# Low halves of the routed rows made by VectorE instead of GpSimd, and GpSimd's loop over the scatters without other work in it

## The reference

```python
h = _L0_tok_ref(x, tok_w, tok_b)            # keep 88 of 125 tokens in each of 32 batches
h = h + _L0_attn_ref(_layernorm(h), ...)    # attention with quantised activations
h = h + _L0_ffn_ref(_layernorm(h), ...)

def _L0_ffn_ref(x, scale, gate_w, gate_b, w1, b1, w2, b2):   # E = 16 experts, K = 4
    t = xf * rsqrt(mean(xf * xf) + EPS) * scale
    g = t @ gate_w.T + gate_b
    vals, idx = top_k(g, K)
    w = softmax(vals) / K
    full_w = zeros((T, E)).at[arange(T)[:, None], idx].set(w)
    h = _swiglu(einsum('th,ehf->tef', t, w1) + b1)
    y = einsum('tei,eih->teh', h, w2) + b2
    return x + einsum('teh,te->th', y, full_w) * K
```

## Time and profile before

| | us |
|---|---|
| median of 3 runs | 892.26 |
| lowest, highest run | 891.8, 892.93 |
| the profiled execution's own time | 891.94 |
| its span | 890.2 |

### The profile page before, as it was taken

One profiled execution on the slowest core, in us unless ns is written; L12 is line 12 of the kernel. 1 busy time (PEld: TensorE's weight loads), 2 busy tenths in 40 slices (PEclk: granted clock), 3 DMA queues, 4 the chain that ended last, 5 costly groups with the idle time before them and its releaser, 6 DMA issues.

```text
span 890.2 us, 16237 instructions
## 1 busy us (share of the span) xinstructions
PE 414.2 (47%) x4049; PEld 283.5 (32%) x4050; DVE 646.5 (73%) x1921; ACT 514.6 (58%) x838; POOL 480.5 (54%) x598
## 2 busy tenths in 40 slices
PE   0476454545454544442230001007887977888300
PEld 0232232323232322222120001005766766766200
DVE  4684769898999898999774226005988978988376
ACT  0242599999999999998520005005665655665200
POOL 8452525554545463626137777771877666776600
PEclk9987655555555555555555555557999998999655
DMA  8499080637271814000001111223434333332186
GB/s 177 51 261 284 2 266 10 186 91 218 58 226 48 259 38 144 1 1 1 0 10 60 65 63 60 76 72 80 115 98 114 92 93 89 96 99 69 27 286 211
DMA packets 102393, 93.37 MB, mean 105 GB/s; under 512 B 14822, under 2 KB 96493, under 8 KB 102338
## 3 DMA queue, kind: packets, MB, share of 16 engines
q1 hardware_dynamic: 88938, 72.87, 29.5%
q0 software_dynamic: 10272, 17.70, 5.8%
q10 hardware_dynamic: 3128, 2.16, 0.8%
HBM read 35.21 MB, written 61.24 MB: 108 GB/s over the span
## 4 chain that ended last, share of the span: by engine, by line
DVE 27%; issue 23%; ACT 19%; PE 12%; POOL 10%; DMA 4%; SPq 3%; DVEq 1%; POOLq 0%; ACTq 0%
POOL region L610 8%; PE pS L1589 3%; DVE S_rho L1091 2%; DMA S_e<-expert_rows 2%; ACT S_sq L784 2%; ACT arena L720 2%; DVE S_ratio L1071 2%; ACT L784 2%; DVE xsel L1349 2%; ACT S_sq L789 2%; DVE arena L1324 2%; ACT pTs L772 2%; DVE stage L1303 2%; DVE arena L1294 2%; PE pP L1589 2%
## 5 line engine op out<-in xcount | busy, mean ns | idle before, releaser
L635 POOL DMA_INDIRECT expert_rows<-stage,dest x118 | 117.8, 998 | 30.0 <-issue 29.1
L610 POOL DMA_INDIRECT region<-arena,slots x96 | 93.9, 979 | 31.7 <-issue 28.1
L491 POOL TENSOR_TENSOR w1s<-stage,w1s 128x384 f16<-128x384 f32 (+17 forms) x72 | 69.7, 968 | 15.1 <-POOL w1s L491 6.3
L582 POOL CAST oq<-o 128x384 bf16<-128x384 int8 x24 | 20.3, 846 | 97.6 <-ACT o L751 97.6
L628 POOL TENSOR_TENSOR stage<-arena,stage 128x256 f16<-128x256 f32 x59 | 40.9, 693 | 52.1 <-ACT stage L849 51.9
L1407 PE MATMUL pX<-arena,WA 128*128 128x384 f16 x86 | 35.3, 514 | 52.0 <-ACT arena L720 49.3
L1613 PE MATMUL pX<-w2s,stage 128*128 x472 | 57.6, 253 | 3.4 <-DVE avE L1305 1.7
L849 ACT ACTIVATE stage<-arena 128x256 f16<-128x256 f32 x59 | 24.6, 417 | 59.0 <-DVE arena L1324 59.0
L1598 PE MATMUL pO<-idh,arena 128*128 128x128 f16 x354 | 31.3, 228 | 50.4 <-DMA arena<-region 49.4
L562 POOL CAST arena<-arena 128x384 bf16<-128x384 int8 x42 | 27.6, 671 | 41.0 <-ACT arena L720 41.0
L808 ACT ACTIVATE arena<-arena 128x576 f16<-128x576 f32 x8 | 5.5, 682 | 75.7 <-DMA region<-arena,slots 71.9
(11 more groups left out here) (356 smaller groups left out, 1833.8 us busy)
## 6 DMA issues: line engine op xcount, KB each, us to landing
region<-zrow SPq DMA_DIRECT2D x45, 800.0 KB
arena<-region SPq DMA_DIRECT2D x59, 200.0 KB
stage<-expert_rows SPq DMA_DIRECT2D x16, 384.0 KB, 4.8
stage<-in_L_ffn_w_dram SPq DMA_DIRECT2D x24, 192.0 KB
stage<-in_L_ffn_w_dram SPq DMA_DIRECT2D x8, 384.0 KB
arena<-in_x_dram SPq DMA_DIRECT2D x4, 672.0 KB
expert_rows<-stage,dest POOLq DMA_INDIRECT x118
out_dram<-xsel ACTq DMA_DIRECT2D x8, 198.0 KB
```

The costliest lines, as they stand in the source:

```text
L491: pool.tensor_tensor(ws[rows, min(kind + 1, 3), two, to:to + width], st[rows, :, at:at + width], ws[rows, kind, two, to:to + width], ALU.s ...
L610: pool.indirect_dma_start(region_rows, bass.IndirectOffsetOnAxis(ap=slots[r][:, i, m:m + 1], axis=0), rows[r][:, i, :].bitcast(I16), None, ...
L635: pool.indirect_dma_start(y_dram, bass.IndirectOffsetOnAxis(ap=dest[(st - 7) % 8][:, j:j + 1], axis=0), ysb[b][:, j, :], None, bounds_chec ...
```

## The change

The two low halves of each group are made on DVE, at a place in DVE's loop between `evac_tT(q-1)` and `top_experts(q-2)`. POOL's loop holds the scatters alone, group after group. Waits, buffers, operands and shapes are the same.

```diff
@@ pool @@
-            def low_rows(q):
-
-                pool.wait_ge(s["high2"], q + 1)
-                low_halves(pool, rows[q % 4], tn[q % 2], s["low2"])
-
             def scatter_rows(q):
...
             pool.wait_ge(s["rows_zeroed"], 16 * NFILL + 64)
-            for q in range(NQ + 3):
-                if q < NQ:
-                    low_rows(q)
-                if q >= 3:
-                    scatter_rows(q - 3)
+            for q in range(NQ):
+                scatter_rows(q)
@@ vector @@
+            def low_rows(q):
+
+                dve.wait_ge(s["high2"], q + 1)
+                low_halves(dve, rows[q % 4], tn[q % 2], s["low2"])
+
             def evac_tT(q):
...
                     norm_rows(q)
                 if 1 <= q < NQ + 1:
                     evac_tT(q - 1)
+                if q < NQ:
+                    low_rows(q)
                 if 2 <= q < NQ + 2:
                     top_experts(q - 2)
                 if q >= 3:
                     find_slots(q - 3)
```

## The result

The changed kernel takes 902.7 us in the median of four runs (901.3 to 904.2), the kernel before beside it 892.0 (890.3 to 892.9). The ratio is 1.0122, with a 95% interval of 1.0100 to 1.0144: slower by 10.7 us. The profiled execution took 902.8 us, with a span of 900.7.

A forecast was written before the change was run, and what follows sets the result against it. The stretch of POOL's 96 scatters was taken to bound the kernel's route; four gaps longer by 3.08 us (+12.3) and the start (+1.1) made +13.4, so 905.6 us, range 901.8 to 908.8.

The forecast's parts named there:

- The mechanism: At groups 1 to 4, DVE's wait for high2 stands ahead of the slots POOL needs, so four gaps remain, each longer.
- The terms of the gap: Between groups on POOL: landing 1.45, ACT 0.68, handover 0.05, halves 0.83, experts and slots 2.95, issue 0.90; 6.86 instead of 3.78 us.
- Halves: In each gap, the pair of low halves on DVE takes 0.83 us, bounds 0.6 and 1.4.
- Experts and slots: In each gap, top_experts and find_slots on DVE up to slots_ready take 2.95 us, bounds 2.8 and 3.1.
- Issue: In each gap, POOL's issue from slots written to first transfer lies open: 0.90 us, bounds 0.75 and 0.98.
- The start: Before the first scatter, DVE's added halves lengthen its chain: +1.1 us, bounds -0.5 and +2.5.
- Nothing else moves: Expert steps start later but keep their length; lower-clock windows may shift them some 1 us either way.
- ACT's wait for the landing: Sign in the changed profile: ACT's L808 still waits for the landing, now some 22 us; 19 us before.
- A: Rival: slots are in hand before DVE's wait, so the four gaps vanish; 879.5 us; chance 4%.
- B: Rival: POOL prepares the transfer before its wait is met, issue 0.1 to 0.3 us; 903 us; chance 10%.
- C: Rival: experts need gates PE makes after the new halves, 2.0 us more per gap; 913.8 us; chance 5%.
- D: Rival: shorter landing and overlap with ACT keep gaps near 3.8 us, time within 0.2%; chance 3%.

The follow-up runs named there:

- Slots ahead of the wait: The changed kernel with DVE's wait and halves moved behind top_experts and find_slots of the same iteration: 877.97 us, ratio 0.9851; repeated 877.08 us, 0.9847.
- second pair: Kernel before and changed kernel, each unaltered and profiled once more in another job: 890.46 us for the kernel before, 903.25 us for the changed one, ratio 1.0136.
- wait-alone run: The kernel before, halves still on POOL, with only DVE's wait for high2 added ahead of top_experts: 897.14 us, ratio 1.0063; repeated 897.00 us, 1.0071.
- kernel with eight buffers: The changed kernel with eight instead of four buffers for rows and slots, dropping ACT's and DVE's waits for row_sent: 879.03 us, ratio 0.9864.
- the halves between experts and slots: The changed kernel with DVE's wait and halves between top_experts and find_slots: 904.41 us on the slow device, then 894.00 us elsewhere, ratio 1.0036 both times.
- the fastest version: The changed kernel with eight buffers and slots made one iteration earlier: 874.79 us, ratio 0.9816; on the slow device 897.77 us, 0.9982.

## Why the prediction was right, point by point

**The mechanism** held: the waiting DVE holds back the slots, and POOL runs dry in the four places where it stood before. Slots ahead of the wait took the gaps away; the wait without the work brought 5.9 of the 6.5 us; moving the wait past the experts took just these out; and with nothing to wait for, the same order made no gap.

**The terms of the gap** were 6.86 in sum and measured 6.55. Halves: 0.83 forecast, 0.74 measured. The two durations came out nearly exactly (0.36 and 0.55 for 0.353 and 0.555); the overlap of some 0.08 came twice, as the next instruction too starts before the second half ends, and the forecast counts it once. Experts and slots: 2.95 forecast, 2.85 measured; L1213 took 0.26 in the row that I read and 0.16 here, as in the two other rows of it. Issue: 0.90 forecast, 0.80 measured, nearer to the row of the steps. Four gaps give 1.2 us less than the sum had. The bounds for four gaps are added up wrongly in the prediction: its own bounds of the terms give gaps of 6.33 to 7.66, so 10.2 to 15.5 us more in four, where it has 8.5 to 15. The measured 11.1 lies in both.

**The start**: +1.1 forecast, +0.56 measured (16.29 to 16.85; 16.28 to 16.86 in the second pair). The COPY takes 0.17 in both places, as the layout had it. The halves, shorter by 0.09 in each of the four iterations up to the first slots, make up most of the difference. The rule of the Trainium skill, "SBUF — State Buffer", section "SBUF: two separate sides", that DVE and GpSimd hold a shared pair of ports from each other for the length of an instruction, again agrees. The small COPY ends 0.02 to 0.03 us after the half that POOL was at when it began: 456.06 after L314's end at 456.03 in the kernel before, and 480.43 after L313's end at 480.41 in the wait-alone run. So it lost 0.44 in one and 0.07 in the other, by how much of POOL's instruction was left. The transfers that DVE's halves lengthened in the kernel with eight buffers are the other direction that the prediction spoke of; in the changed kernel no transfer starts within a half, as it had said.

**Nothing else moves** was wrong by a little. The steps were 1.1 us longer in the first pair of profiles and 1.6 in the second, which I had only as chance. Against it, the route began 2.1 us sooner in the profiled execution (0.7 in the second pair). These, with the gaps and the start, are the 2.9 us between the forecast of 905.6 and 902.7. Route alone, forecast +13.4, measured +11.4. The earlier start of the route lies ahead of everything that the change touches, so that it offsets the longer steps is luck. Among the signs, ACT's wait for the landing was to grow to some 22 us; it was 19.1 at the first gap and 18.6 at the others, against 19.0 and 17.6 to 17.7. The first has no longer gap before it, and before the others ACT's `exp_gates` now starts 2.7 us after its high part, where it was 1.0.

**The rivals.** A, the gaps vanish, needed the slots ahead of the wait, and that kernel gave 878.0 where A had 879.5. B, the issue hidden, is refuted by 0.80 us in each gap. The time alone would not have told: 902.7 lies nearer to B's 903 than to 905.6. C, PE in the gap: no L1167 stands between halves and experts. D: the landing is 1.45 as it was.

## What to carry to other kernels

A piece of work that is moved to an idle engine takes its waits along, and in an in-order queue everything behind them waits too: ask not what the moved work costs but what stands behind its wait, and who needs that. Here the work was 0.74 us and the wait cost three times as much, and the same move with the call behind `top_experts` and `find_slots` is worth 14 us. An engine that looks idle may already be waiting for the same thing: DVE did, one iteration later, when the slots that POOL needed next were already made. Where an engine feeds another that is the bound, put what the bound needs ahead of any wait on the bound's own results, or take away what there is to wait for.

## What the runs showed of the hardware that was not expected

- A scatter from GpSimd that has to wait for its semaphore starts 0.80 us after the semaphore's writer has ended, in the gaps that slots end (the change, the wait alone, the halves between experts and slots), and 0.97 to 1.04 us at the first scatter of all. Where the wait was met earlier, this is hidden, and the idle time is 0.17 after other work and 0.30 in a run of scatters.
- Halves on DVE beside GpSimd's transfers, in the kernel with eight buffers, lengthened three transfers from 0.97 to 1.26, 1.11 and 1.29, with 0.42, 0.27 and 0.44 us of the half left at their start; the fastest version has four such (1.27, 1.12, 1.30, 1.11 with 0.42, 0.28, 0.45, 0.27 left). With slots ahead of the wait four transfers start with 0.10 to 0.12 left and take 0.97. The 96 scatters took 122.6 us with eight buffers against 121.8 with slots ahead of the wait.
- On one device the kernel before took 900.3 us in place of 892, and DVE had waits of up to 14 us that the profile puts down to no engine of the core. What they are is open. They showed in both kernels profiled there and in none of the twelve profiles from elsewhere, the two of the kernel before and the two of the change among them.
- The expert steps, untouched, took 234 to 238 us according to the kernel, and repeated within 0.8 us for each of the four kernels profiled twice away from that one device (the kernel before, the change, the wait alone, slots ahead of the wait). This was not tried further.
